# A new timetable for the five queues of a four-layer convolution and attention kernel

## What is computed

```python
# layer 0: depthwise 3x3 and 1x1 for q, k, v; keys and values resized to 7x7; attention with a bias table; again
# depthwise and 1x1; residual; then an MLP with a residual
out = batchnorm(x, ...); q, k, v = split(dsconv(out, w_qkv_dw, w_qkv_pw))
k, v = bilinear_to_7(k), bilinear_to_7(v)
o = softmax((q @ k + bias) * SCALE) @ v
out = dsconv(o, w_out_dw, w_out_pw) + x
x = einsum(relu(batchnorm(out)), w_mlp) + out
# layer 1: group norm; keys softmaxed over channels, queries over points; linear attention; projection; + xn
xn = group_norm(x); q, k, v = split(xf @ qkv_w.T + qkv_b)
context = einsum('bnc,bnd->bcd', softmax(k, -1), v); out = softmax(q, -2) @ context @ proj_w.T + proj_b
x = out + xn
# layer 2: group norm; attention with 8 heads over 196 points; projection; residual
a = softmax(scale * q @ k) @ v; x = x + proj_w @ a + proj_b
# layer 3: group norm; attention with one head of 256 channels over 196 points; projection; residual
attn = softmax(q @ k * c ** -0.5); x = x + wo @ (v @ attn) + bo
```

## Time and profile before

| | |
|---|---|
| median of 3 runs | 2128.81 us (2125.54 to 2136.21) |
| profiled execution, span | 2132.0 us |
| PE, ACT, DVE, POOL busy | 94%, 88%, 87%, 62% |
| mean granted clock of TensorE | 0.978 |
| one turn in the level part (v0 on PE to the next v0) | 61.90 us |

### The profile page before, as it was taken

How to read it: one execution, slowest core, us unless ns; L and a number is a source line. 1 busy time by engine, 2 the same in 40 slices (tenths; PEclk the granted TensorE clock), 3 DMA queues, 4 the chain that set the end, 5 groups by cost and what they waited for, 6 DMA issues and landing times.

```text
span 2132.0 us, 60375 instructions
## 1 busy us (share of the span) xinstructions
PE 2014.2 (94%) x15232; PEld 1692.3 (79%) x15232; DVE 1851.5 (87%) x4683; ACT 1883.5 (88%) x6231; POOL 1313.0 (62%) x2954
## 2 busy tenths in 40 slices
PE   5578999999999999999999999999999999999977
PEld 3367788888888888888888888888888888888766
DVE  6778999999999999999999999999999999997532
ACT  2258999999999999999999999999999999999984
POOL 3554667676666767676676666666667666664321
PEclk8699999999999999999999999999999999999988
DMA  3000011011001101110110011011001101000000
GB/s 128 15 24 9 32 40 40 17 38 38 31 29 38 38 15 38 38 38 23 38 38 24 29 38 38 23 38 38 30 23 38 38 23 38 31 32 18 23 24 38
DMA packets 29823, 70.34 MB, mean 33 GB/s; under 512 B 6252, under 2 KB 7088, under 8 KB 29744
## 3 DMA queue, kind: packets, MB, share of 16 engines
q1 hardware_dynamic: 26928, 67.68, 9.1%
q10 hardware_dynamic: 2816, 1.72, 0.3%
HBM read 30.85 MB, written 12.85 MB: 20 GB/s over the span
## 4 chain that ended last, share of the span: by engine, by line
PE 80%; DVE 8%; ACT 5%; issue 4%; POOL 2%; SPq 1%; DVEq 1%; DMA 0%; POOLq 0%; ACTq 0%
PE ps_e L1176 19%; PE ps_c L1176 19%; PE ps_b L1176 15%; PE ps_a L1176 10%; PE ps_s L1176 9%; PE ps_s L1231 6%; DVE y L1168 3%; DVE y L1149 1%; ACT e L839 1%; PE ps_a L1478 1%; DVE x L1088 1%; ACT e L831 1%; DVE m L1113 1%; DVE y L1163 1%; ACT pt L845 1%
## 5 line engine op out<-in xcount | busy, mean ns | idle before, releaser
L831 ACT ACTIVATE e<-ps_s,nm 98x196 f32<-98x196 f32 x1024 | 426.5, 447 | 44.4 <-DVE nm L967 43.2
L839 ACT ACTIVATE e<-e,rden 98x196 f32<-98x196 f32 x1024 | 408.4, 477 | 1.1 <-DVE rden L1072 1.0
L596 POOL TENSOR_SCALAR xn<-x,gn_scale,gn_shift 128x196 f32<-128x196 f32 x384 | 308.3, 813 | 20.8 <-POOL gn_shift L591 20.8
L1168 DVE SCALAR_TENSOR_TENSOR y<-opad,w_dw,y 128x406 f32<-128x406 f32 x512 | 313.4, 664 | 0.0
L1149 DVE SCALAR_TENSOR_TENSOR y<-xpad,w_dw,y 128x406 f32<-128x406 f32 x512 | 300.8, 641 | 0.0
L967 DVE TENSOR_REDUCE nm<-ps_s 98x4 f32<-98x784 f32 x256 | 239.5, 967 | 34.8 <-PE ps_s L1176 34.8
L845 ACT COPY pt<-ps_s 98x392 f32<-98x392 f32 x512 | 237.2, 509 | 7.6 <-PE ps_s L1231 4.1
L1231 PE MATMUL ps_s<-w_eye,e 98*98 98x98 f32 x2048 | 229.1, 250 | 8.5 <-ACT e L839 8.2
L831 ACT ACTIVATION_READ_ACCUMULATOR e<-ps_s,nm 98x1 f32 x1024 | 233.6, 228 | 0.0
L1231 PEld LDWEIGHTS ps_s<-w_eye,e 98*98 98x98 f32 x2048 | 201.1, 130 | 39.5 <-issue 23.5
L574 POOL TENSOR_TENSOR gn_t<-gn_group 128x4 f32<-128x4 f32 x96 | 26.6, 277 | 312.5 <-DVE gn_group L1017 222.7
(11 more groups left out here) (227 smaller groups left out, 5569.6 us busy)
## 6 DMA issues: line engine op xcount, KB each, us to landing
x_in<-in_x SPq DMA_DIRECT2D x32, 392.0 KB, 3.3
x_res<-in_x SPq DMA_DIRECT2D x32, 392.0 KB, 3.2
x2b<-x SPq DMA_DIRECT2D x32, 392.0 KB, 2.7
out<-x SPq DMA_DIRECT2D x32, 392.0 KB, 2.6
out_pairs<-out SPq DMA_DIRECT2D x32, 392.0 KB, 2.5
w_q<-in_q SPq DMA_DIRECT2D x3, 256.0 KB
w_k<-in_k SPq DMA_DIRECT2D x3, 256.0 KB
w_v<-in_v SPq DMA_DIRECT2D x3, 256.0 KB
```

Of the source, the lines that this page charges most:

```text
L596: g.tensor_scalar(dst[:, c, of_image(i)], src[:, c, of_image(i)], t.scale[:, j:j + 1], t.shift[:, j:j + 1], ALU.mult, ALU.add).then_inc(t. ...
L831: s.activation(e2[:, j, tc], tile(use)[0:HALF, of_image(tc)], ACT.Exp, bias=nm2[:, j, tc:tc + 1], accum_out=den2[:, 2 * i + tc, h:h + 1]). ...
L839: s.activation(e2[:, j, tc], e2[:, j, tc], ACT.Copy, scale=rden2[:, 2 * i + tc, h:h + 1]).then_inc(p2_done[j].sem, 1)
L1168: v.scalar_tensor_tensor(out=dst, in0=window(opad, c, k, CR), scalar=tap, in1=dst, op0=ALU.mult, op1=ALU.add).then_inc(conv2_steps.sem, 1)
```

## The change

The tables PE_AT, ACT_AT, DVE_AT and POOL_AT have new numbers, and BANK_USES deals the plain products to the four banks anew. SP_AT is the same. No instruction is added or taken away. The order of the steps on POOL and SP stays; on PE, ACT and DVE it is new. Five steps get another lag: `bn0`, `bn1` and `conv1_0` come one turn earlier; `t3_0` on ACT and `o3_1` on PE one turn later. Of guards that depend on the numbers only the name of a last reader changes (`out0` for `out1` on POOL, `hq1` for `hk1` and `v3_0` for `v3_3` on ACT), and `hv1` on ACT no longer has one.

Cut to the parts that the text speaks of:

```diff
 PE_AT = {
-    "q0_1": 102, ... "v0": 176, "t0_0": 178, ...
-    "o0_0": 187, "pw0": 254, "pw1": 268, "mlp0": 283, "mlp1": 284, "gn1": 302, "kv0": 340, "kv1": 342, "kv2": 346,
-    "kv3": 349, "q1_0": 353, "q1_1": 356, ... "sc1": 466, "av0": 472, "tn1_1": 483,
-    ... "proj1": 587, "proj0": 593, ...
-    "q3_1": 658, "v3_1": 659, "v3_2": 663, "q3_0": 670, "v3_0": 672, "v3_3": 674, ...
-    "t3_0": 731, "t3_1": 757, "o3_1": 764, "o3_0": 778,
+    "q0_1": 107, ... "v0": 172, "t0_0": 176, ...
+    "o0_1": 195, "pw0": 252, "pw1": 257, "mlp0": 283, "mlp1": 284, "gn1": 301, "kv0": 352, "kv1": 354, "kv2": 355,
+    "kv3": 360, "q1_0": 361, "q1_1": 362, ... "tn1_1": 494, "sc1": 478, "av0": 487,
+    ... "proj1": 605, "proj0": 607, ... "v3_2": 658,
+    "v3_1": 660, "q3_1": 661, "q3_0": 669, "v3_3": 675, "v3_0": 683, ...
+    "t3_0": 762, "o3_1": 772, "o3_0": 783,
 }

 ACT_AT = {
-    "bn0": 9, "bn1": 12, ... "v0": 185, ... "high1_0": 336, "high1_1": 340, "kv0": 350, ...
-    "tn0_1": 459, "tn0_0": 462, "tn0_3": 465, "tn0_2": 466, "hk1": 467, "hv0": 470,
-    "sc1_0": 473, "sc1_1": 475, "sc1_2": 476, "sc1_3": 477, "less1_0": 481, ...
-    "v3_1": 672, "v3_2": 674, "v3_0": 686, "v3_3": 689, "s3_0": 708, "probs3_0": 727, "s3_1": 728, "probs3_1": 760, ...
+    "bn0": -39, "bn1": -7, ... "v0": 183, ... "high1_0": 334, "high1_1": 337, "kv0": 354, ...
+    "hv0": 456, "tn0_0": 463, "hk1": 464, "tn0_3": 469, "tn0_2": 470, "tn0_1": 471,
+    "sc1_1": 476, "sc1_0": 477, "sc1_3": 479, "sc1_2": 480, "less1_0": 481, ...
+    "v3_2": 664, "v3_1": 666, "v3_3": 693, "v3_0": 696, "s3_0": 728, "s3_1": 730, "probs3_0": 731, "probs3_1": 734, ...
 }

 DVE_AT = {
-    "conv1_0": 12, "conv1_1": 14, "conv1_2": 46, "conv1_3": 48, "conv1_4": 53, "conv1_5": 54, "conv1_6": 57,
-    "conv1_7": 62, "conv1_8": 70, ... "conv2_0": 196, "conv2_1": 201, "conv2_2": 232, "conv2_3": 237, ...
-    "stats1": 299, "gn1": 301, "low1_0": 330, "low1_1": 334, "kv0": 338, "kv1": 340, "kv2": 346, "rk0": 349,
-    "kv3": 352, "rk1": 354, ... "gn2": 390, ... "gn3": 604, "low3_0": 649, ... "s3_0": 696, ...
+    "conv1_0": -2, "conv1_1": 11, "conv1_2": 22, "conv1_3": 47, "conv1_4": 52, "conv1_5": 56, "conv1_6": 57,
+    "conv1_7": 61, "conv1_8": 73, ... "conv2_0": 191, "conv2_1": 195, "conv2_2": 199, "conv2_3": 227, ...
+    "stats1": 300, "gn1": 302, "low1_0": 328, "low1_1": 330, "kv0": 345, "kv1": 346, "rk0": 352, "rk1": 356,
+    "kv2": 357, "kv3": 358, ... "gn2": 393, ... "gn3": 610, "low3_0": 648, ... "s3_0": 691, ...
 }

 POOL_AT = {
-    "resize0": 96, "resize1": 112, "probs0": 160, "probs1": 176, "gn1": 336, "gn2": 400, "gn3": 640, "rows3": 704,
+    "resize0": 96, "resize1": 112, "probs0": 149, "probs1": 181, "gn1": 336, "gn2": 400, "gn3": 640, "rows3": 704,
 }

 BANK_USES = {
-    "a": ("t0_1", "o0_1", "gn1", "ctx0", "hv0", "gn3", "v3_2", "v3_0", "t3_0", "t3_1", "o3_1",),
-    "b": ("k0", "v0", "o0_0", "mlp0", "q1_0", "ctx1", "out1", "v3_1", "v3_3", "s3_1",),
-    "c": ("q0_0", "s0_0", "pw0", "kv1", "kv3", "q1_1", "hq0", "hq1", "hk1", "q3_0", "s3_0", "o3_0",),
-    "e": ("q0_1", "s0_1", "t0_0", "pw1", "mlp1", "kv0", "kv2", "out0", "gn2", "hk0", "hv1", "proj1",
-          "proj0", "q3_1",),
+    "a": ("pw1", "ctx0", "hq0", "proj0", "gn3", "q3_1", "s3_0", "t3_1", "o3_0",),
+    "b": ("q0_0", "s0_0", "v0", "kv0", "q1_0", "gn2", "hv1", "proj1", "v3_2", "q3_0", "t3_0",),
+    "c": ("k0", "o0_0", "pw0", "mlp1", "kv2", "q1_1", "ctx1", "out1", "hk0", "hv0", "hq1", "v3_1", "v3_0", "s3_1",),
+    "e": ("q0_1", "s0_1", "t0_0", "t0_1", "o0_1", "mlp0", "gn1", "kv1", "kv3", "out0", "hk1", "v3_3", "o3_1",),
 }
```

## The result

2241.64 us median of 4 runs (2240.54 to 2245.03) against 2129.57 us for the kernel before, beside which it ran: a ratio of 1.052 (95% interval 1.050 to 1.055). The change makes the kernel 112 us slower; I had said 2180, and no more than 2224.

A forecast was written before the change was run, and what follows sets the result against it. PE bounded the old kernel at 61.9 us a turn; the new order's round through all engines, 52.6 plus 11.2 for gn1, made 63.8. 27 turns of 1.9 gave 51 us more: 2180, range 2127 to 2224.

The forecast's parts named there:

- Step 1: PE from q0_1 to v0: 34.8 us of the new round, against 34.43 in the old order.
- Step 2: v0 on PE, then ACT's four copies of v0 and v3_0's copy: 2.6 us with the hand-overs.
- Step 3: POOL's rows3, waiting for v3_0's read and standing ahead of gn1: 0.9 us with hand-overs.
- Step 4: POOL's gn1 up to its second image, then ACT's high1_0: 11.2 us, stretched by DVE's taps.
- H: Time of POOL's gn1 up to its second image, the forecast's unknown: 11.2 us taken, bounds 7.5 and 12.6.
- Steps 5 and 6: ACT from high1_0 to kv0, 10.4 us; then kv0's exponential, DVE up to kv3, and q0_1 on PE, 3.9 us.
- 27 turns: Turns 5 to 31, in which all links have a pair; each 1.9 us longer, 51 us in all.
- A: Faster: PE stays the bound at 61.1 us a turn, the kv0 wait gone; 2105 us, chance 0.10.
- B: No change to tell: gn1 takes 8.9 to 9.7 us or a second round decides; 2118 to 2139 us, chance 0.13.
- C: Slower still: gn1 blocked as before at 12.6 us, gn2 holding up high2_0; 2218 to 2235 us, chance 0.17.
- The spare of the old round: Old order's round over gn1 summed to 58.0 us, 3.9 us inside the turn.
- The kv0 wait: PE's kv0 waits behind DVE's read of proj0, 0.62 us a turn; the new banks were to remove it.

The follow-up runs named there:

- two repairs: Kernel after the change with v3_0 ahead of v0 on ACT and conv1_8 ahead of low1_0 on DVE: 2227.64 us, ratio 1.042.
- the last two kernels: Kernel before the change with kv0 in bank a and some ten single steps moved, two versions: 2127.45 and 2124.97 us, ratios 0.996 and 0.995.

## Why the prediction was wrong, step by step

The direction, the place (the round over rows3 and gn1, in the level part) and the size of the unknown were right; the sum of the round was 1.2 us short, and the clock was left out. Against the round of 64.98 us at the full clock (the rows of the second and third step are those of the turn shown first):

- Step 1, PE from q0_1 to v0: 34.8 said, 34.75 measured. Right. The seams are in the rows: six products of 128x392 take 1.16 to 1.18 us from their start to the next group's between groups of the other number type, and 1.07 within a run of their own. But the 0.2 a turn that I took for them does not show in PE's whole turn: without its idle time it is 61.2 before, and 61.4 with v3_0 first and with short taps, where I had 61.1.
- Step 2, v0 on PE to the end of v3_0's copy: 2.6 said, 2.56 measured (919.34 to 921.90). Right.
- Step 3, rows3: 0.9 said, 1.50 measured (921.90 to 923.40). Mis-sized: its two instructions take 0.72, where I had 0.75, but POOL begins the first 0.71 after the copy's end, where I had put 0.15 for all hand-overs (the row names t0_0's copy, for which rows3 does not wait; the gap is 0.70 as well where v0's copies follow v3_0). In the old order that gap was 0.38. A likely reason, not tested: POOL waits for three banks' last v3 copies in turn, v3_0's first, so that two more waits stand behind the late one; in the old order the late copy, v3_3, was waited for last.
- Step 4, H: 11.2 said, 11.00 measured. Right, with its cause: the half-length taps gave 8.43. In the new order no step of gn1 was held up for more than one DVE instruction (its longest step took 0.57 to 0.72 us in the turns of the level part, a tap's half 0.64); so here the trace agrees with the Trainium skill (SBUF — State Buffer, section "SBUF: two separate sides"), whose rule I had put at 10.8, and the long block of the earlier trace rows, which every level turn of the old order has (3.08 to 3.14), did not come back.
- Steps 5 and 6, high1_0 to q0_1: 14.3 said, 15.16 measured. This is the step that failed as a way. I followed ACT from high1_0 to kv0's exponential. The other follower of high1_0 is low1_0 on DVE, and behind it DVE has ten us of work without a hole up to kv1, whose bank kv3 needs. I had named low1_0 as waiting, and did not go on along its queue.
- "PE will stand some 5% of each turn; ... I cost the clock at nothing." This failed: 0.6 us a turn in the kernel after the change, and 1.4 in the one with two repairs. The row that I rested on the earlier trace rows is a share of a long stretch; it does not say how long PE stands in one piece. I also missed where it would stand: at sc1, for the copies of tn0 that the change had put behind high1_0, 2.72 us at once.
- 27 turns: right. Ramp and tail, 0 with 10 either way: 9. By the tables eight steps and not five change their lag: out1 on DVE and sc2_0 and sc2_1 on ACT as well, which moved a few places across the edge of a turn.

Added up: 63.8 - 0.05 - 0.04 + 0.60 - 0.20 + 0.86 = 64.97, and 0.6 for the clock makes the mean turn of 65.58. 27 x 1.8 = 49 and 9 of the ramp and tail are 58 of the 62 us by which 2180 missed.

The rivals: A and B had the old bound or gn1 done early, and neither came. C gave 2218 to 2235, nearest to the result, by a blocked gn1 (H of 12.6) and gn2; that was not the reason, since H was smaller than in my own forecast, and in a level turn ACT waits for POOL's images only at high1_0 and, for 0.05, at one other place. Of the signs, high1_0's wait (2.59), low1_0's behind it (2.76), gn1 right after rows3 (923.33 to 923.40) and kv0 without its wait came as told; q0_1's wait for kv3 did not (at the full clock, with the tn0 copies first, DVE has read kv3 0.2 us ahead of q0_1, so the way by kv3 was close), and PE's 54.5 of 57 busy came out at 53.89, though with slow work in it. The spare of the old round was about 2.0 and not 3.9. The kv0 wait on which A rested can be had in the old order, at 61.2 a turn in the last two kernels; in the new order no run came under 62.40, so that 61.1 could be reached there is not shown.

## What to carry to other kernels

When a step gets late, follow each queue that waits for it to the end, and the fullest one first: the round is as long as its longest way, and here DVE's unbroken queue behind low1_0 beat the way by ACT that I had summed. Where a change makes TensorE stand still, ask how long it stands in one piece and read the granted clock in stretches of a microsecond behind that place; a share over a long stretch hides it. A step that runs on POOL beside vector work should be begun early and have spare, because a tap moved out of one queue's way can cost nearly as much by slowing the POOL step beside it.

## What the runs showed of the hardware

The granted clock turned small differences of order into large ones. After a wait of 1.50 us ahead of sc1 it stayed at 1.00 and the kernel took 2191 us; after one of 2.44, with nearly the same order, it fell to 0.50 in each turn, for 2228. The length of one wait does not settle it: in the kernel before with two Newton steps more the clock fell around waits of 2.1 to 2.2 in all but two of the steady turns, and with the tn0 copies first it fell four times in turns whose longest wait was 1.5. Filling part of the wait with work without use took 14 us and 36 us off. And two Newton steps, 3.2 us a turn, cost the kernel before 100 us, where one step, 1.3 us, cost nothing.
